# Cross-attention over 12544 keys: half of the key rows kept whole in the first pass and split by the vector engine in the second, with a reordered opening

## The reference, cut to what matters

```
x = x + xattn(layernorm(x), ctx)        # 16 heads, 12544 keys, softmax over all of them
x = x + causal_self_attention(layernorm(x))
x = x + gated_ffn(layernorm(x))         # 768 hidden, weights and activations rounded to grids
```

## Time and profile before

| | us |
|---|---|
| median of 3 runs (lowest, highest) | 483.58 (482.57, 485.65) |
| the profiled execution | 485.21, span 483.5 |
| busy in the span: PE, DVE, ACT, POOL | 455.1, 275.6, 384.4, 99.6 |
| granted TensorE clock, mean | 0.979 |
| DMA | 117.5 MB, mean 243 GB/s |

### The profile page before, as it was taken

One profiled execution on the slowest core, in us unless ns is written; L12 is line 12 of the kernel. 1 busy time (PEld: TensorE's weight loads), 2 busy tenths in 40 slices (PEclk: granted clock), 3 DMA queues, 4 the chain that ended last, 5 costly groups with the idle time before them and its releaser, 6 DMA issues.

```text
span 483.5 us, 15996 instructions
## 1 busy us (share of the span) xinstructions
PE 455.1 (94%) x6464; PEld 357.4 (74%) x6464; DVE 275.6 (57%) x406; ACT 384.4 (80%) x436; POOL 99.6 (21%) x101
## 2 busy tenths in 40 slices
PE   8799999999999999996899999999999999999896
PEld 4666667666676666672588999999999999985463
DVE  5579999999999999999479400000000000004566
ACT  7678888888888888875378999999999999993423
POOL 1598532343334333305000000000000000000000
PEclk9989999999999999997789999999999999999999
DMA  8986667866668766958918877777888777500000
GB/s 263 357 335 219 262 228 292 327 241 241 256 245 327 283 238 260 379 227 315 414 57 327 326 246 263 285 269 275 301 327 309 268 263 265 209 3 2 1 1 14
DMA packets 34986, 117.50 MB, mean 243 GB/s; under 512 B 4240, under 2 KB 10768, under 8 KB 34960
## 3 DMA queue, kind: packets, MB, share of 16 engines
q1 hardware_dynamic: 30784, 110.58, 60.7%
q0 software_dynamic: 4032, 6.42, 4.4%
q10 hardware_dynamic: 144, 0.13, 0.1%
HBM read 74.44 MB, written 39.47 MB: 236 GB/s over the span
## 4 chain that ended last, share of the span: by engine, by line
PE 46%; DVE 5%; ACT 1%; issue 1%; ACTq 0%; DVEq 0%
PE ps_a L1045 21%; PE ps_k L1058 19%; DVE early L727 1%; PE ps_a L1215 1%; PE ps_k L1232 1%; PE ps_a L942 1%; PE ps_k L1094 0%; PE ps_a L1142 0%; ACT middle L573 0%; PE ps_a L1122 0%; ACT early L559 0%; PE ps_a L1202 0%; DVE small L808 0%; PE ps_a L1194 0%; DVE early L817 0%
## 5 line engine op out<-in xcount | busy, mean ns | idle before, releaser
L691 DVE TENSOR_REDUCE block_max<-ps_a 128x2 f32<-128x896 f32 x112 | 121.2, 1084 | 0.2 <-PE ps_a L931 0.2
L1045 PEld LDWEIGHTS ps_a<-q_stack,k_stack 64*128 64x128 f32 x1568 | 98.6, 191 | 14.8 <-issue 12.7
L1045 PE MATMUL ps_a<-q_stack,k_stack 64*128 64x128 f32 x1568 | 107.9, 283 | 1.0 <-issue 0.5
L488 ACT CAST early<-ps_a 128x896 bf16<-128x896 f32 x104 | 94.7, 911 | 6.0 <-PE ps_a L931 6.0
L559 ACT ACTIVATE early<-ps_a 128x1536 f32<-128x1536 f32 (+1 forms) x56 | 90.3, 1662 | 10.4 <-PE ps_a L1045 10.4
L559 ACT ACTIVATE middle<-ps_a 128x1536 f32<-128x1536 f32 (+1 forms) x56 | 90.4, 1663 | 8.5 <-PE ps_a L1045 8.5
L759 DVE COPY early<-ps_k 128x256 f32<-128x256 f32 x2 | 0.8, 420 | 164.4 <-PE ps_k L1058 164.4
L897 PE MATMUL ps_a<-w_hi,k_stack 128*128 128x256 f32 x392 | 69.0, 298 | 0.0
L888 PE MATMUL ps_k<-k_stack,w_hi 128*128 128x448 f32 x224 | 60.8, 392 | 4.9 <-POOL k_stack L379 4.3
L696 DVE TENSOR_TENSOR early<-early 128x896 bf16<-128x896 bf16 x104 | 64.2, 618 | 0.0
L897 PEld LDWEIGHTS ps_a<-w_hi,k_stack 128*128 128x128 f32 x392 | 53.4, 190 | 11.4 <-issue 11.4
(11 more groups left out here) (188 smaller groups left out, 434.5 us busy)
## 6 DMA issues: line engine op xcount, KB each, us to landing
k_stack<-k_hi_scratch SPq DMA_DIRECT2D x56, 448.0 KB, 6.1
v_scratch<-early SPq DMA_DIRECT2D x14, 952.0 KB, 5.5
v_in<-v_scratch SPq DMA_DIRECT2D x14, 952.0 KB, 7.8
k_hi_scratch<-k_hi SPq DMA_DIRECT2D x28, 448.0 KB, 2.8
k_lo_scratch<-k_lo SPq DMA_DIRECT2D x28, 448.0 KB, 3.3
k_stack<-k_lo_scratch SPq DMA_DIRECT2D x28, 448.0 KB, 5.9
ctx_b<-in_ctx SPq DMA_DIRECT2D x7, 896.0 KB, 7.6
early<-in_ctx SPq DMA_DIRECT2D x6, 896.0 KB, 7.5
```

What stands on the lines that cost most here:

```text
L488: nc.scalar.copy(staged[:, u % 2], pair_scores(u, 0)).then_inc(max_copied, 1)
L691: nc.vector.tensor_reduce(block_max[:, 2 * u:2 * u + 2, par], pair_scores(u, 1), AX.X, ALU.max).then_inc(max_taken, 1)
L1045: last = nc.tensor.matmul(ps_a[:, base + bank, at * Q:(at + 1) * Q], k_stack[half, b_par, a, t * P:(t + 1) * P], q_stack[half, a, ab, :], ...
```

## The change

In the first pass, `split_first(s, m)` tells which keys are still split: m = 0 always, m = 1 only in blocks 0 and 1 (WHOLE = 2). For the others `low_keys` is left out on DVE, ACT writes the sum whole as float32, SP stores it once, and PE's next projection of keys waits for ACT alone (`hi_ready`). In the second pass the whole keys are loaded into slots 1, 2 and 3, and DVE then rewrites the four rows of m = 1 in place. For each row it makes an instruction that writes `signed` = key x `hi_sign` + slot-0 flag, rounded, and one that writes key x slot-2 flag + `signed` over the row, which is the high part, the low part or one by slot. PE waits for that (`stack_split`). There are three stack buffers (BUFS = 3): the third lies where `k_full`, `k_lo` and a context buffer lie in the first pass and is filled with ones by two ACT instructions of 128 x 3584 once the last stores have landed. Block b + 1 is loaded where block b was. DVE's work on the feed-forward weights is interleaved with the splits of blocks 3 to 6. The second pass is written out for six blocks in a loop of two rounds, and once for two.

In the opening PE sums the flag ahead of spreading the queries, the key projection of slot 8 moves behind the first unit of scores, DVE reduces both halves of the mask ahead of its second key split, and ACT copies the first scores ahead of that slot's key evacuation and of two context pieces.

```diff
+BUFS = 3
+WHOLE = 2
+RAW = PR // 2
...
+        stacks = sb("stacks", [P, BUFS, PR, BK], f32r)
+        k_full = third[:, 0:2 * DC * BK].rearrange("p (b m k) -> p b m k", b=2, m=DC)
...
+        def split_first(s, m):
+            return m == 0 or isinstance(s, int) and s < WHOLE
...
             def store_keys(s, par, m):
                 sp.wait_ge(hi_ready, (s * DC + m + 1) * 2)
-                sp.dma_start(k_hi_d[s, m], k_hi[:, par, m, :].bitcast(f32)).then_inc(hi_stored[par][m], 16)
-                sp.wait_ge(lo_ready, (s * DC + m + 1) * 2)
-                sp.dma_start(k_lo_d[s, m], k_lo[:, m, :].bitcast(f32)).then_inc(lo_stored[m], 16)
+                sp.dma_start(k_d[s, m], k_full[:, par, m, :]).then_inc(hi_stored[par][m], 16)
+                if split_first(s, m):
+                    sp.wait_ge(lo_ready, low_keys_done(s, m, 1))
+                    sp.dma_start(k_lo_d[s, m], k_lo[:, m, :]).then_inc(lo_stored[m], 16)
...
+                for m in (1, 0):
                     for slot in range(1, STRIDE):
-                        src = (k_lo_d if slot == 2 else k_hi_d)[b, m]
+                        src = (k_lo_d if slot == 2 and split_first(b, m) else k_d)[b, m]
...
+            sp.wait_ge(third_filled, DC)
+            load_keys(2)
+
             sp.wait_ge(row_max_ready, NB + 1)
...
-            with sp.Fori(1, NB // 2) as i:
-                for par in range(2):
-                    b = i * 2 + par
+            for b in range(2, NB):
+                if b + 1 < NB:
                     sp.wait_ge(scored, (b - 1) * UNITS)
-                    load_keys(b, par)
-                    sp.wait_ge(prob_slots_free, (b - 1) * UNITS + SLOTS_P)
-                    load_values(b, par)
+                    load_keys(b + 1)
+                sp.wait_ge(prob_slots_free, (b - 1) * UNITS + SLOTS_P)
+                load_values(b)
...
-                            high_piece(1, 1, 2)
-                            high_piece(1, 1, 3)
+                            copy_scores(0, 0)
...
+                    if first and slot == H - 2 * LAG:
+                        high_piece(1, 1, 2)
+                        high_piece(1, 1, 3)
...
+            act.wait_ge(max_scored, NB * NG)
+            for m in range(DC):
+                for par in range(2):
+                    act.wait_ge(hi_stored[par][m], 16 * NB // 2)
+                act.wait_ge(lo_stored[m], 16 * (WHOLE if m else NB))
+            act.wait_ge(ctx_split, NB * PIECES)
+            for m in range(DC):
+                nc.scalar.activation(stacks[:, 0, m * PR // 2:(m + 1) * PR // 2, :].rearrange("p a (n k) -> p (a n) k", n=2),
+                                     zeros_b[:, 0:HK].unsqueeze(1).to_broadcast([P, PR, HK]), ACT.Identity,
+                                     bias=ones_c[:]).then_inc(third_filled, 1)
...
             ask_flag(0)
+            ask_flag(1)
             low_keys(0, 0, 0, 1)
-            ask_flag(1)
+            dve.wait_ge(flag_summed, 1)
...
-                    if work[0] == "k":
+                    if work[0] == "k" and split_first(s, work[1]):
                         low_keys(s, par, work[1], work[2])
...
+            def round_row(b, n):
+
+                done = (b - WHOLE) * RAW + n
+                if done >= len(signed):
+                    dve.wait_ge(stack_split, RAW + done - len(signed) + 1)
+                nc.vector.tensor_scalar(signed[done % len(signed)], stacks[:, (b + 1) % BUFS, PR - RAW + n, :].bitcast(f32),
+                                        hi_sign[:], slot_is[:, 0:1], ALU.mult, ALU.add).then_inc(rounded, 1)
+
+            def split_stack(b):
+
+                arrived(b, 1)
+                round_row(b, 0)
+                for n in range(RAW):
+                    if n + 1 < RAW:
+                        round_row(b, n + 1)
+                    done = (b - WHOLE) * RAW + n
+                    dve.wait_ge(rounded, done + 1)
+                    row = stacks[:, (b + 1) % BUFS, PR - RAW + n, :]
+                    nc.vector.scalar_tensor_tensor(row, row.bitcast(f32), slot_is[:, 2:3], signed[done % len(signed)].bitcast(f32),
+                                                   ALU.mult, ALU.add).then_inc(stack_split, 1)
...
+                    if split_first(last_s, last_m):
+                        pe.wait_ge(lo_ready, low_keys_done(last_s, last_m, last_n))
+                    else:
+                        pe.wait_ge(hi_ready, (s * DC + m) * 2 + n)
...
+            pe.wait_ge(flag_asked, 2)
+            for n in range(2):
+                last = nc.tensor.matmul(ps_a[0:1, 3, 0:1], flag_f[:, n:n + 1], ones_c[:], start=(n == 0), stop=(n == 1))
+            last.then_inc(flag_summed, 1)
             pe.wait_ge(x3_ready, DC)
...
-            project(0, 0, 8)
...
                 score_for_max(0, 0, 0, masked)
+                project(0, 0, H - 2 * LAG)
...
+                def arrive(b, j):
+                    pe.wait_ge(stack_in[j % BUFS][0], (b - j) * 16 + j // BUFS * 48 + 48)
+                    pe.wait_ge(stack_split, b * RAW)
...
-                with pe.Fori(0, NB // 2 - 1) as i:
-                    two_blocks(i, False)
-                two_blocks(NB // 2 - 1, True)
+                period = 2 * BUFS
+                with pe.Fori(0, NB // period) as i:
+                    blocks(i * period, period, False)
+                blocks(NB // period * period, NB % period, True)
```

More of the change, by code:

```diff
@@ L167, in perceiver_layer @@
         v_stored = [sem(f"v_stored{i}") for i in range(2)]
-        stack_in = [sem(f"stack_in{i}") for i in range(2)]
+        stack_in = [[sem(f"stack_in{i}{m}") for m in range(DC)] for i in range(BUFS)]
         v_back = [sem(f"v_back{i}") for i in range(2)]
@@ L471, in evacuate_keys @@
                     act.wait_ge(hi_stored[par][m], (s - par) * 8)
-                nc.scalar.activation(k_hi[:, par, m, n * HK:(n + 1) * HK], ps_k[:, 0:HK], ACT.Identity,
+                keys = k_full[:, par, m, n * HK:(n + 1) * HK]
+                nc.scalar.activation(keys.bitcast(f32r) if first or m == 0 else keys, ps_k[:, 0:HK], ACT.Identity,
                                      bias=bk[:, m:m + 1]).then_inc(hi_ready, 1)
@@ L522, in evacuate @@
                                                      bias=bqs[:, m:m + 1], scale=HD ** -0.5).then_inc(x3_ready, 1)
+                    if first and slot == H - 2 * LAG:
+                        high_piece(1, 1, 2)
+                        high_piece(1, 1, 3)
                     of_last, u = scored_in(slot)
-                    if not (of_last and first):
+                    if not first or slot > H - 2 * LAG:
                         copy_scores(s - of_last, u)
@@ L753, in _ @@
             nc.vector.transpose(w_raw[:, DC * F:2 * DC * F], w_raw[:, 0:DC * F]).then_inc(weights_ready, 1)
+            for b in range(7, NB):
+                split_stack(b)
             dve.wait_ge(bv_in, 16)
@@ L974, in _ @@
             last.then_inc(q_projected, 1)
-            pe.wait_ge(flag_asked, 2)
-            for n in range(2):
-                last = nc.tensor.matmul(ps_a[0:1, 3, 0:1], flag_f[:, n:n + 1], ones_c[:], start=(n == 0), stop=(n == 1))
-            last.then_inc(flag_summed, 1)
-            project(0, 0, 8)
             pe.wait_ge(flag_ready, 1)
@@ L1061, in add_up @@
                     last.then_inc(prob_slots_free, 1)
-                def arrive(b, par):
-                    pe.wait_ge(stack_in[par], (b - par) * 48 + 96)
+                def arrive(b, j):
+                    pe.wait_ge(stack_in[j % BUFS][0], (b - j) * 16 + j // BUFS * 48 + 48)
+                    pe.wait_ge(stack_split, b * RAW)
                     if masked:
-                        pe.wait_ge(mask_t_in[par], (b - par) * 8 + 16)
-                def two_blocks(i, final):
-                    for u in range(0, 2 * UNITS, 2):
-                        ending = final and u == 2 * UNITS - 2
+                        pe.wait_ge(mask_t_in[j % 2], (b - j % 2) * 8 + 16)
@@ L1073, in two_blocks, with blocks @@
+                def blocks(first, count, final):
+                    for u in range(0, count * UNITS, 2):
+                        ending = final and u == count * UNITS - 2
                         for w in (u, u + 1):
                             if not ending:
-                                pe.wait_ge(exp_done, i * (2 * UNITS) + w + 1)
-                                nxt = (w + 2) % (2 * UNITS)
-                                if nxt == 0:
-                                    arrive(i * 2 + 2, 0)
@@ L1079, in two_blocks @@
[L1079 to L1082 removed]
+                                pe.wait_ge(exp_done, first * UNITS + w + 1)
+                                j, unit = divmod(w + 2, UNITS)
+                                if unit == 0:
+                                    arrive(first + j, j)
@@ L1088, in two_blocks @@
                             add_up(w // UNITS, w % UNITS, w % SLOTS_P)
-                arrive(0, 0)
+                for m in range(DC):
+                    pe.wait_ge(stack_in[0][m], 48)
```

(2 more changed lines are left out.)

125 lines of the change are left out of this document (73 added, 52 removed).

## The result

The changed kernel took 497.12 us (median of 4 runs, 496.37 to 498.43) beside 483.07 of the kernel before (478.08 to 485.65). The ratio is 1.0329, with a 95% interval of 1.0245 to 1.0414. I had forecast 477.5 in a range of 471.5 to 482.5: wrong in sign and by 20 us. (Ratios here leave out disturbed runs, two of four of `b_six`, one of them its profiled execution, and three of nine of `b_six_light`, so that these two medians lie above what the ratios say.)

What follows compares the result with a forecast made beforehand. DVE was taken as full in the first pass and PE as always busy in the second. Terms -4.5 - 1.0 - 1.0 + 0.4 = -6.1 us gave 477.5 us against the median of 483.6, range 471.5 to 482.5.

Steps and rivals of the forecast that it cites:

- (7): Second pass on PE: a few instruction stops in four more written-out blocks, +0.4 us (0 to +2).
- The slower one: Rival, second pass: DVE becomes the bound and PE waits for the split stack, 488.4 us; chance 7%.
- (1): First pass: dropped m = 1 splits end PE's wait for GpSimd, 0.41 us in each of 11 joins, 4.5 us gained.
- The collision of GpSimd and DVE: Rival, first pass: DVE gets in first and delays GpSimd's quarter, 3.3 us of the gain lost, 480.8 us; chance 18%.
- (3): Opening: reordered work lets ACT copy the first scores earlier, -1.0 us (+0.5 to -2.0); GpSimd's later pieces cost PE nothing.
- (4): Middle: DVE's lag goes and ACT's two fills, 6.5 us, fit the wait for the rows, -1.0 us (0 to -1.2).
- The clock in the middle: Rival, 236 to 246 us: a shorter gap before the scores keeps the clock up, 4.5 us more gained, 473.0; chance 19%.
- (6): Second pass: DVE's splits take 7 to 8 us a block and stay covered, 0 us.
- (2): First pass stores: SP loses 12 stores and 12 waits on DVE, which PE does not feel, 0 us.
- (5): Second pass loads: keys issued one block earlier and ahead of the feed-forward weights, 0 us.
- faster by more: Chance 0.61 of a clear gain: 0.39 from the forecast, 0.19 from the held clock, 0.04 from DVE's full price.

Runs made afterwards that it cites:

- b_six: Kernel before with only PE's second pass written out for six blocks in a loop of two rounds and two more: 503.79 us, ratio 1.0384.
- b_six_light: `b_six` with the key loads of blocks 2 to 13 cut from 896 columns to 128: median 489.21 us, ratio 1.0109.
- a_nosplit: Changed kernel with DVE's split in the second pass cut from 896 columns to 2, waits kept: 499.28 us, ratio 1.0404.
- b_four: Kernel before with PE's second pass in a loop of three rounds of four blocks and two more: 509.84 us, ratio 1.0607.
- a_straight: Changed kernel with PE's second pass written out for all 14 blocks, no loop: 481.16 us, ratio 1.001.
- b_open: Kernel before with the change's new opening alone: 484.06 us, ratio 1.0064.
- b_lowcut: Kernel before with DVE's low split of m = 1 in blocks 2 to 13 cut to 2 of 448 columns: 475.77 us, ratio 0.9925.
- b_straight: Kernel before with PE's second pass written out for all 14 blocks, no loop: 484.13 us, ratio 1.0105.
- a_two: Changed kernel with two stack buffers, a two-block PE loop, earlier key loading, no ACT fills, DVE rows split in two column parts: 477.16 us, ratio 0.9941.
- a_two_old: `a_two` with the opening of the kernel before: 476.13 us, ratio 0.9929.

## Why the prediction was wrong

**(7), PE's code: the step that failed.** I priced four more written-out blocks at +0.4, by the one stop of 0.55 in the kernel before, and closed the range at +2. It cost +20.8. The row was read as what new code costs. It came from the only new code in that loop, the first round of a body that is then held: no packet of instructions comes from 270 to 410. Two things were never in the row. The jump back to a body that is no longer held costs 9.2 us (5.9 standing, 3.3 behind it), and 8.7 to 10.1 in `b_six`, `a_nosplit` and `b_four`. And the fetches themselves beside a DMA share of 0.7 to 0.8 cost another 12 here and 5 in `a_straight`. Both bounds came from a row that couldn't hold the mechanism, and the row that could have warned me isn't among mine: the 19 packets of the instruction queue, against 14 blocks of 672 instructions, which at 249 a packet would be 38 for the second pass alone. None of my rivals had it either. The slower one was given 7% and named DVE; PE never waits for DVE's split there.

**(1), the first pass: right in mechanism, 1.6 too high (4.5 for 2.9).** -2.9 against -4.5. GpSimd's wait is gone, the wait for ACT ahead of the last scores is still 0.42, and one block of two does take 14.40. On PE, and on DVE the folds of four blocks in a row:

```profile
129.90 0.38 PE L1011 MATMUL ps_a<-third,q_pair 32*128 32x448 bf16 x4 [0.42 <-ACT early L507]
130.50 0.67 PE L968 MATMUL ps_k<-stacks,w_hi 128*128 128x448 f32 x2 [0.23 <-issue]
```

```profile
111.03 0.18 DVE L733 TENSOR_TENSOR block_max<-block_max 128x16 f32<-128x16 f32 x1
...
125.42 0.18 DVE L733 TENSOR_TENSOR block_max<-block_max 128x16 f32<-128x16 f32 x1
...
140.10 0.18 DVE L733 TENSOR_TENSOR block_max<-block_max 128x16 f32<-128x16 f32 x1
...
154.51 0.18 DVE L733 TENSOR_TENSOR block_max<-block_max 128x16 f32<-128x16 f32 x1
```

14.39, 14.68, 14.41. The 0.3 in every second block is the first pass's own jump back on PE, 0.23 before 130.50; it had run under GpSimd's wait. 11 blocks at 0.26 are the 2.9. The collision of GpSimd and DVE (18%) did not happen in a size that counts: DVE's L727 takes 0.61 us alone and took 0.70 at 126.51, where a GpSimd instruction had begun 0.93 ahead of it.

**(3), the opening: wrong, and small.** +0.7 in the two profiles where I took -1.0. Two profiles can't tell that: over all of this document the first fold of block 1 comes at 49.8 to 53.4 us in seven profiles with the old opening and at 51.4 to 53.1 in five with the new one. `b_open` with its 12 runs says not faster. I followed ACT and PE and let GpSimd's later pieces pass as free ("PE does not wait for it here"); PE waits 1.42 for them.

**(4), the middle: right.** -1.2 against -1.0. The two fills (6.46 against my 6.5) cover the wait for the rows almost exactly:

```profile
223.73 0.91 ACT L507 CAST early<-ps_a 128x896 bf16<-128x896 f32 x1 [0.67 <-PE ps_a L1011]
224.53 6.46 ACT L572 ACTIVATE stacks<-zeros_b,ones_c 128x3584 fp32r<-128x3584 bf16 x2
231.08 1.07 ACT L579 ACTIVATE q_stack<-ps_a 1x512 fp32r<-1x512 f32 x2
```

**The clock in the middle (rival, 19%): it happened,** for 4.2 us against my 4.5. The rival's reason, the gap shortened by 1.2 us, is not what decides: `b_lowcut` has 8.65 us from the warm-up matmuls to the first scores, for 9.51, and its clock fell. What goes with it in the twelve profiles is PE's stop ahead of turning the maxima into rows: 1.38 in the kernel before and 1.03 to 1.85 in the four others whose clock fell, 0.39 in the changed kernel and at most 0.81 in the six others whose clock held, among them `b_straight` and `b_six_light` with the old middle. No run changed that stop alone. And the clock is less the change's gain than the ledger makes it look. Of the 29 runs of the kernel before beside `a_two`, 10 had a mean clock of 0.993 and took 477.4 to 479.7; those at 0.982 or less took 481.6 to 484.8. So the kernel before sometimes holds its clock, and its profiled execution (0.979) was one that did not. `a_two` and `a_two_old` were at 0.986 or more in all 24 runs. At 0.993 `a_two_old` took 474.1 to 474.9.

**(6), DVE's splits: right.** The two instructions a row, over the second pass:

```profile
L801 DVE SCALAR_TENSOR_TENSOR stacks<-stacks,slot_is,early 128x896 fp32r<-128x896 f32 x16 | 18.4, 1147 | 0.0
...
L788 DVE TENSOR_SCALAR early<-stacks,hi_sign,slot_is 128x896 fp32r<-128x896 f32 x16 | 11.9, 743 | 20.6 <-DMA stacks<-k_scratch 19.0 <-issue 1.6
```

4 rows at the spacing of a pair, 1.72, are 6.9 us a block (forecast 7 to 8). **(2) and (5)**, stores and loads, show no wait of PE on a queue. (The chances for faster by more, 0.39, 0.19 and 0.04, add up to 0.62 and not 0.61; nothing hangs on it.)

What stays open: why the stop in the middle differs from run to run of one kernel, which length of body between 1344 and 2688 instructions is the last that is held, for which two bodies in that gap would have to be tried, and what makes up the 3.3 us that a jump still stands with half the data.

## What to carry to other kernels

Count the instructions of a loop's body on its busiest engine before writing it out further, and read the packets of the instruction queue: if they are as many as the rounds times the body, each jump back waits for a fetch, here 3.3 to 6.8 us and the clock after it. When a third buffer forces a longer body, try two buffers with finer waits first. And a cost whose nearest row comes from code that is held is no bound for code that isn't.

## What the runs showed of the hardware that I had not expected

- A jump back on PE costs at most 0.3 us when the body is held (five of them are in the 160 us of `a_two_old` in which PE was idle for 0.12), 5.7 to 6.8 us when it isn't and the DMA share inside the stop is 0.97 to 1.02 (`b_six`, `a_nosplit`, `b_four` and the changed kernel), and 3.3 when it is 0.70 (`b_six_light`).
- Behind the stop of 5.88 us the granted clock fell, to 1.2 GHz of 2.4 by the next 84 matmuls, which took 6.44 us for 3.66; behind the one of 1.76 its mean over 6 us was 0.72. With stops of 0.48, 0.87 and 0.62 in it, the window from 340 to 400 has 1.00.
- Straight code that is fetched once and in order stops PE 5 times in 14 blocks, 2.9 us together, beside a DMA share of 0.78.
